# A two-layer graph network: layer 1 sums its messages in bfloat16, as three exact pieces side by side

## The chip, the core and the metric

The kernel runs on one core of one Trainium2 chip. The metric is the device time of one execution in microseconds (us), lower is better. Before the change three runs took 4851.73, 4855.97 and 4856.16 us; the median is 4855.97 us.

The engines are named as the profile names them: PE is TensorE (PEld its weight loads), DVE is VectorE, ACT is ScalarE, POOL is GpSimd, SP is SyncE.

## What is computed

Two message-passing layers over a graph of 6250 nodes and 200000 edges, sorted by target. `src` is an edge's source node and `dst` its target. Cut to what matters:

```python
h = relu(layernorm(x))                              # (6250, 128)
# layer 1: attention with 8 heads of 16 numbers
z = (h @ W).reshape(N, 8, 16)
e = leaky_relu(el[src] + er[dst], 0.2)              # el, er: one number per node and head
a = exp(e - emax[dst])
agg = segment_sum(z[src] * a[:, :, None], dst)      # the sum that is changed
out = agg / segment_sum(a, dst)[:, :, None] + bias
x = x + out
# layer 2: per-edge products of a node's row with edge attributes and a small MLP of the
# edge's features, again summed by target, and a linear map; x = x + that
```

## The kernel before

The edges are cut into 196 groups of 1024 (8 columns of 128 edges, one edge on each partition). Both layers walk the 196 groups in 49 rounds of 4 (slots s = 0 to 3). A group's work in layer 1 is as follows.

- **POOL** gathers the source rows of the group: 8 indirect DMAs (line 436), each of 128 rows of 144 float32 numbers, from the table `z_tab` in DRAM into `rows`, slot s. A row holds, per head, 16 numbers of z and a 1 (so that the same sum gives the denominator), in all MW = 136 numbers, and 8 numbers `el`. Before the 8 gathers of group g it waits (line 461) until PE has signalled `agg` of group g - 2, the summing matmuls below. In this layer POOL does nothing else.
- **PE** copies the targets' numbers out over the partitions (`spread`, line 1161, two matmuls of 512 columns), two groups ahead; **ACT** turns this into a transposed one-hot (lines 527 and 530); **PE** fetches the targets' `er` with it (line 1170, 8 small matmuls, signalled as `er`), also two groups ahead.
- **DVE**, once the rows have landed: adds `el` and `er` (941, 942), takes the maximum (946), writes the one-hot of the *next* group (862: 128x1024), and, once **ACT** has taken the exponential (551), forms the message in two halves of 4 columns (956: 128x544 each), signalled as `msg0` and `msg1`. Then it reduces the next group's `er` (869) and adds the previous group's sums from PSUM into an accumulator in SBUF (876: 128x136).
- **PE** sums: for each of the 8 columns a matmul with the one-hot of 128x128 float32 as weights and 136 columns of the message (1213). The last one signals `agg`.

After slot 1 of a round DVE finishes those blocks of 128 nodes that are complete (`finish_block`, lines 886 to 916, 49 in all, about one in a round): divide, add to x, layernorm, a transpose and a matmul on PE (1184, 1187), each of which DVE waits for (910, 915). The row goes to the table `up_tab` for layer 2, which SP stores.

Layer 2 has the same frame (8 gathers a group, from `up_tab`), with DVE products (1052 to 1069) and its own sums on PE (1278). It can't begin to gather before the last block of layer 1 has been stored.

The order on each engine is the order in which it is written; nothing plans it. Each engine runs its own loop, and semaphores tie them.

Of the kernel before, what the change touches and what calls it, by code (L numbers as in the profile page):

```python
# [8 lines left out]
BF16 = mybir.dt.bfloat16  # L9
# [4 lines left out]
P = 128  # L14
# [51 lines left out]
def gnn_kernel(nc, x, src, dst, dst_lin, edge_y, edge_f, bias, front, weights, out):  # L66

    with ExitStack() as ctx:
# [31 lines left out]
        acc = sb("acc", [P, 4 * COLS])  # L100
# [18 lines left out]
        hotT = lay(U * GE, GE).bitcast(BF16).rearrange("p (h e) -> p h e", h=2)  # L119
# [14 lines left out]
        assert PARTS_AT + 2 * GE <= 4 * COLS and (U + 1) * GE <= COLS  # L134
# [77 lines left out]
        msg = part(0, 2, T, MW)  # L212
# [47 lines left out]
        def slot_sems(tag, names):  # L260
# [5 lines left out]
                                                         "exp", "msg0", "msg1", "agg", "added", "rows"))  # L266
# [342 lines left out]
        def _(dve):  # L609
# [251 lines left out]
            def one_hot(s, group):  # L861
                v.tensor_tensor(hot[:, s, :, :],  # L862
                                bc(dst_col[:, bass.ds(group, 1), :].rearrange("p a t -> p (a t)"), 2, P),
                                bc(iota_l1, 1, T), ALU.is_equal)
# [8 lines left out]
            def add_sums(s, at):  # L873

                to = sums_at[:, bass.ds(at, 1), :].rearrange("p a f -> p (a f)")
                v.tensor_tensor(to, to, bank[2 + s % 2][:, 0:MW], ALU.add).then_inc(s_l1["added"][s], 1)
# [43 lines left out]
            with dve.Fori(0, passes1) as k:  # L920
# [5 lines left out]
                v.memset(bank[3][:, 0:MW], 0.0)  # L926
                with dve.Fori(0, GI) as q:
                    n = dve.snap(k * GI + q + 1, min_val=1, max_val=PASSES1 * GI)
                    m = dve.snap(k * QUADS + q + 1, min_val=1, max_val=PASSES1 * QUADS)
                    m_1 = dve.snap(k * QUADS + q + 2, min_val=2, max_val=PASSES1 * QUADS)  # L930
                    landed = dve.snap(q * (16 * T) + 16 * T, min_val=16 * T, max_val=GI * 16 * T)
# [4 lines left out]
                    for s in range(U):  # L936
# [17 lines left out]
                        for hf in range(2):  # L954
                            ts = slice(hf * HT, hf * HT + HT)
                            v.scalar_tensor_tensor(  # L956
                                out=msg[:, h, ts, :].rearrange("p t (h f) -> p t h f", f=RW),
                                in0=bc(a_ps[h][:, ts, :], 3, RW), scalar=1.0,
                                in1=rows[:, s, ts, 0:MW].rearrange("p t (h f) -> p t h f", f=RW),
                                op0=ALU.min, op1=ALU.mult).then_inc(s_l1["msg0" if hf == 0 else "msg1"][s], 1)  # L960
# [7 lines left out]
                        add_sums((s - 1) % U, slots[s])  # L968
# [6 lines left out]
                add_sums(3, last)  # L975
# [125 lines left out]
        def _(pe):  # L1101
# [90 lines left out]
            with pe.Fori(0, passes1) as k:  # L1192
# [7 lines left out]
                with pe.Fori(0, GI) as q:  # L1200
# [5 lines left out]
                    for s in range(U):  # L1206
# [3 lines left out]
                        for i in range(T):  # L1210
                            if i % HT == 0:
                                pe.wait_ge(s_l1["msg1"][s] if i else s_l1["msg0"][s], n)
                            mm = t.matmul(bank[2 + h][:, 0:MW], hot[:, s, i, :], msg[:, h, i, :],  # L1213
# [154 lines left out]
```

## Time and profile before

| | |
|---|---|
| median of the timed runs | 4855.97 us |
| the profiled execution | 4860.6 us, its span 4858.4 us |
| busy share of the span | POOL 62%, PE 58%, DVE 52%, PE weight loads 42%, ACT 21% |
| DMA engines | under 20% busy in both layers |
| layer 1's gathers | from about 0.12 ms to 2.42 ms |
| layer 2's gathers | from 2.45 ms to the end |

Shares of busy time are means over both layers. A gap before an instruction is printed in brackets with what ended it; "remote" and "another core or an unknown queue" both mean that the profile has no instruction of this core whose recorded end fits. The ends of matmuls are modelled.

### The profile page before, as it was taken

The page shows a single profiled execution, that of the slowest core. Times are in us where ns is not written, and L with a number is a line of the kernel's source. Part 1 is how long each engine was busy: PE and PEld are TensorE (multiplying, and loading weights), DVE is VectorE, ACT ScalarE, POOL GpSimd, SP SyncE. Part 2 cuts the span into 40 slices and gives each one's busy share as a digit, 9 for nine tenths or more (in the row PEclk, how much of TensorE's full clock was granted, in tenths as well). Part 3 has the DMA queues.
Part 4 walks back from the last instruction along what each step waited for, and adds up shares of the span by engine and source line. Part 5 has one row for each costly group of instructions (what it writes and reads, how often), then busy time and mean ns, then how long its engine had stood idle before and what let it go on. Part 6 is the DMA issues. An engine that isn't in the chain of part 4 may idle for free.

```text
span 4858.4 us, 43517 instructions
## 1 busy us (share of the span) xinstructions
PE 2816.5 (58%) x11218; PEld 2050.7 (42%) x11219; DVE 2517.3 (52%) x6576; ACT 1018.9 (21%) x1447; POOL 3030.4 (62%) x3146
## 2 busy tenths in 40 slices
PE   2444444444444444444467777777777777777776
PEld 2333333333333333333345545455555554445454
DVE  7333333333434334333356666666666666666565
ACT  3222222222222222222221111111111111111111
POOL 2666666666666666666656666666666666666665
PEclk8665666566666566666678888888888888888888
DMA  3111111111111111111111111111111111111111
GB/s 104 50 51 49 52 49 52 52 52 48 52 52 51 52 53 51 52 52 50 50 43 51 47 49 46 49 48 50 49 51 49 49 50 48 47 49 49 47 47 39
DMA packets 139864, 246.43 MB, mean 51 GB/s; under 512 B 54124, under 2 KB 85974, under 8 KB 139734
## 3 DMA queue, kind: packets, MB, share of 16 engines
q0 software_dynamic: 100352, 218.57, 16.3%
q1 hardware_dynamic: 39352, 26.89, 1.9%
q10 hardware_dynamic: 144, 0.80, 0.1%
q8 instruction: 5, 0.08, 0.0%
q14 instruction: 11, 0.09, 0.0%
HBM read 236.02 MB, written 10.03 MB: 51 GB/s over the span
## 4 chain that ended last, share of the span: by engine, by line
POOL 41%; issue 21%; PE 15%; another core or an unknown queue 15%; DVE 4%; DMA 3%; ACT 1%; DVEq 0%; POOLq 0%; ACTq 0%; SPq 0%
POOL rows L436 41%; PE pair L1278 7%; PE pair L1240 2%; PE pair L1234 2%; DMA rows<-up_tab,idx 2%; PE pair L1230 1%; PE pair L1213 1%; PE pair L1254 1%; ACT share L565 1%; DMA rows<-z_tab,idx 0%; DVE share L1063 0%; DVE share L1057 0%; ACT share L567 0%; PE pair L1126 0%
## 5 line engine op out<-in xcount | busy, mean ns | idle before, releaser
L436 POOL DMA_INDIRECT rows<-up_tab,idx x1568 | 1534.1, 978 | 879.4 <-issue 473.1
L436 POOL DMA_INDIRECT rows<-z_tab,idx x1568 | 1494.9, 953 | 924.9 <-issue 557.4
L1213 PE MATMUL pair<-share,acc 128*128 128x136 f32 x3136 | 755.6, 432 | 1127.2 <-issue 653.8
L1213 PEld LDWEIGHTS pair<-share,acc 128*128 128x128 f32 x3136 | 701.1, 326 | 1263.8 <-issue 720.6
L1278 PE MATMUL pair<-share,acc 128*128 128x256 f32 x3136 | 933.5, 450 | 368.1 <-DVE share L1069 220.1
L1278 PEld LDWEIGHTS pair<-share,acc 128*128 128x128 f32 x3136 | 695.4, 228 | 764.6 <-issue 338.6
L941 DVE TENSOR_TENSOR share<-rows,share 128x64 f32<-128x64 f32 x196 | 46.0, 235 | 1159.2 <-DMA rows<-z_tab,idx 1152.8
L1052 DVE TENSOR_TENSOR share<-rows,y_sb 128x384 f32<-128x384 f32 x392 | 222.3, 567 | 631.9 <-DMA rows<-up_tab,idx 601.0
L1240 PE MATMUL pair<-weights_sb,share 128*128 128x256 f32 x1576 | 412.1, 408 | 130.5 <-ACT share L567 74.3
L1240 PEld LDWEIGHTS pair<-weights_sb,share 128*128 128x128 f32 x1576 | 313.0, 203 | 197.5 <-ACT share L567 87.8
L567 ACT ACTIVATE share<-pair,front_sb 128x512 f32<-128x512 f32 x198 | 136.1, 687 | 1046.3 <-issue 387.6
L551 ACT ACTIVATE pair<-share 128x64 f32<-128x64 f32 x196 | 44.6, 228 | 1441.7 <-DVE share L946 1132.9
L565 ACT ACTIVATE share<-pair,front_sb 128x512 f32<-128x512 f32 x198 | 136.1, 687 | 901.2 <-PE pair L1230 608.3
L1234 PE MATMUL pair<-share,weights_sb 128*128 128x512 f32 x396 | 264.1, 756 | 71.8 <-ACT share L565 71.1
L956 DVE SCALAR_TENSOR_TENSOR share<-pair,rows 128x544 f32<-128x544 f32 x392 | 264.1, 715 | 0.0
L996 DVE TENSOR_TENSOR acc<-acc,pair 128x1024 f32<-128x1024 f32 x197 | 239.8, 1217 | 1.4
L862 DVE TENSOR_TENSOR acc<-acc,pair 128x1024 f32<-128x1024 f32 x197 | 240.3, 1220 | 0.0
L1230 PE MATMUL pair<-ef_sb,weights_sb 64*128 64x512 f32 x396 | 235.9, 677 | 5.0 <-DMA ef_sb<-in_edge_f 4.2
L527 ACT ACTIVATE acc<-pair,acc 128x1024 bf16<-128x1024 f32 x198 | 219.7, 1110 | 90.7 <-remote 73.7
L530 ACT ACTIVATE acc<-acc,ones 128x1024 bf16<-128x1024 bf16 x198 | 227.3, 1148 | 6.4
L1057 DVE TENSOR_TENSOR share<-rows,share 128x384 f32<-128x384 f32 x392 | 219.3, 559 | 0.0
L1063 DVE TENSOR_TENSOR share<-share,y_sb 128x384 f32<-128x384 f32 x392 | 214.5, 547 | 0.0
(166 smaller groups left out, 2416.6 us busy)
## 6 DMA issues: line engine op xcount, KB each, us to landing
rows<-z_tab,idx POOLq DMA_INDIRECT x1568
rows<-up_tab,idx POOLq DMA_INDIRECT x1568
ef_sb<-in_edge_f SPq DMA_DIRECT2D x50, 128.0 KB
z_tab<-rows SPq DMA_DIRECT2D x7, 504.0 KB, 3.2
y_sb<-in_edge_y SPq DMA_DIRECT2D x50, 64.0 KB
x_sb<-in_x SPq DMA_DIRECT2D x7, 448.0 KB, 6.9
up_tab<-acc SPq DMA_DIRECT2D x49, 64.0 KB
out<-x_sb SPq DMA_DIRECT2D x48, 64.0 KB
```

The lines of the kernel that those rows point to most:

```text
L436: pool.indirect_dma_start(out=rows[:, s, t, 0:width], out_offset=None, in_=table, in_offset=bass.IndirectOffsetOnAxis(ap=indices[:, t:t + ...
L527: nc.scalar.activation(to, spread_ps, ACT.Square, bias=minus_id[:, bass.ds(tile, 1)])\
L530: nc.scalar.activation(to, to, ACT.Relu, bias=ones[:, 0:1], scale=-2.0).then_inc(s_l1["turned"][s], 1)
L862: v.tensor_tensor(hot[:, s, :, :], bc(dst_col[:, bass.ds(group, 1), :].rearrange("p a t -> p (a t)"), 2, P), bc(iota_l1, 1, T), ALU.is_equal)
L956: v.scalar_tensor_tensor(out=msg[:, h, ts, :].rearrange("p t (h f) -> p t h f", f=RW), in0=bc(a_ps[h][:, ts, :], 3, RW), scalar=1.0, in1=r ...
L996: v.tensor_tensor(hot[:, s, :, :], bc(dst_col[:, bass.ds(group, 1), :].rearrange("p a t -> p (a t)"), 2, P), bc(iota_l2, 1, T), ALU.is_equal)
L1052: v.tensor_tensor(vy, vecs, y_v, ALU.mult)
L1213: mm = t.matmul(bank[2 + h][:, 0:MW], hot[:, s, i, :], msg[:, h, i, :], start=(i == 0), stop=(i == T - 1))
L1230: t.matmul(bank[4], a1_bd[at, s, :], ef_sb[at, :], start=True, stop=True).then_inc(s_l2["h1"], 1)
L1234: t.matmul(bank[4], a2_bd[:, :], h1_sb, start=True, stop=True).then_inc(s_l2["h2"], 1)
L1240: mm = t.matmul(bank[2 * (s % 2) + j // 2][:, (j % 2) * 256:(j % 2) * 256 + 256], h2_sb[:, s % 2, j * P:(j + 1) * P], a3_bd[:, :], start=T ...
L1278: mm = t.matmul(bank[6 + s % 2][:, 0:MSG], hot[:, s, hf * HT + j, :], msg2[:, s % 2, hf, j, :], start=(hf + j == 0), stop=(hf == 1 and j = ...
```

## The change

Layer 1 only. The one-hot is written as bfloat16 (0 and 1 are exact in it). The float32 message m is split into three pieces, whose bits each fit a bfloat16: the upper half of m's own bits, the upper half of the rest, and the rest of that. The pieces lie side by side as `split[h]`, of shape [128, 3, 8, 136] float32 cells (2 buffers); `upper` is a view of the upper 2 bytes of each cell. Splitting takes four more DVE instructions a group, each reading two operands from `acc`, which is SBUF. `msg0` and `msg1` are signalled by the last two of them. PE then runs 8 matmuls of 3 x 136 = 408 bfloat16 columns, with a bfloat16 one-hot as weights. DVE adds the three sums (a reduction from PSUM into `part_sum`), and then adds that to the accumulator. Three core parts of the diff:

```diff
             def one_hot(s, group):
-                v.tensor_tensor(hot[:, s, :, :],
+                v.tensor_tensor(hot1[:, s, :, :],
...
-            def add_sums(s, at):
-
+            def add_sums(s, at, counted, wait=plain_wait):
+
+                v.tensor_reduce(part_sum, bank[2 + s % 2][:, 0:3 * MW].rearrange("p (c f) -> p f c", c=3), AX.X, ALU.add)\
+                    .then_inc(s_l1["folded"], 1)
                 to = sums_at[:, bass.ds(at, 1), :].rearrange("p a f -> p (a f)")
-                v.tensor_tensor(to, to, bank[2 + s % 2][:, 0:MW], ALU.add).then_inc(s_l1["added"][s], 1)
+                wait(dve, s_l1["folded"], counted)
+                v.tensor_tensor(to, to, part_sum, ALU.add).then_inc(s_l1["added"][s], 1)
...
-                        for hf in range(2):
-                            ts = slice(hf * HT, hf * HT + HT)
+                        by_half = [slice(0, HT), slice(HT, T)]
+                        for ts in by_half:
                             v.scalar_tensor_tensor(
-                                out=msg[:, h, ts, :].rearrange("p t (h f) -> p t h f", f=RW),
+                                out=split[h][:, 0, ts, :].rearrange("p t (h f) -> p t h f", f=RW),
                                 in0=bc(a_ps[h][:, ts, :], 3, RW), scalar=1.0,
                                 in1=rows[:, s, ts, 0:MW].rearrange("p t (h f) -> p t h f", f=RW),
-                                op0=ALU.min, op1=ALU.mult).then_inc(s_l1["msg0" if hf == 0 else "msg1"][s], 1)
+                                op0=ALU.min, op1=ALU.mult).then_inc(s_l1["halved"], 1)
+                        for hf, ts in enumerate(by_half):
+                            dve.wait_ge(s_l1["halved"], halves + (4 * s + hf))
+                            v.tensor_tensor(split[h][:, 1, ts, :], split[h][:, 0, ts, :], upper[h][:, 0, ts, :],
+                                            ALU.subtract).then_inc(s_l1["halved"], 1)
+                        for hf, ts in enumerate(by_half):
+                            dve.wait_ge(s_l1["halved"], halves + (4 * s + 2 + hf))
+                            v.tensor_tensor(upper[h][:, 2, ts, :], split[h][:, 1, ts, :], upper[h][:, 1, ts, :],
+                                            ALU.subtract).then_inc(s_l1["msg0" if hf == 0 else "msg1"][s], 1)
...
-                            mm = t.matmul(bank[2 + h][:, 0:MW], hot[:, s, i, :], msg[:, h, i, :],
+                            mm = t.matmul(bank[2 + h][:, 0:3 * MW], hot1[:, s, i, :], upper[h][:, :, i, :],
```

On DVE, in the loop of layer 1 from the messages of slot 2 to the start of slot 3, the order before is this (`pair2` holds the exponentials, `pair3` the er parts, `pair1` the sums, all in PSUM; `edges_` names the semaphores of the text above):

```order
L956 SCALAR_TENSOR_TENSOR share<-pair2,rows 128x544 [waits edges_exp_slot2]
L956 SCALAR_TENSOR_TENSOR share<-pair2,rows 128x544
L869 TENSOR_REDUCE share<-pair3 128x128 [waits edges_er_slot3]
L876 ISA [waits edges_er_sum_slot3]
L876 TENSOR_TENSOR acc<-acc,pair1 128x136
L941 TENSOR_TENSOR share<-rows,share 128x8x8 [waits edges_rows_slot3]
```

And in the same place of the changed kernel (its own line numbers; `acc` holds the pieces and the accumulator, `share` holds `part_sum`):

```order
L968 SCALAR_TENSOR_TENSOR acc<-pair2,rows 128x544 [waits edges_exp_slot2]
L968 SCALAR_TENSOR_TENSOR acc<-pair2,rows 128x544
L974 REGISTER_ALU
L975 TENSOR_TENSOR acc<-acc 128x544 [waits edges_halved]
L974 REGISTER_ALU
L975 TENSOR_TENSOR acc<-acc 128x544 [waits edges_halved]
L978 REGISTER_ALU
L979 TENSOR_TENSOR acc<-acc 128x544 [waits edges_halved]
L978 REGISTER_ALU
L979 TENSOR_TENSOR acc<-acc 128x544 [waits edges_halved]
L876 TENSOR_REDUCE share<-pair3 128x128 [waits edges_er_slot3]
L882 TENSOR_REDUCE share<-pair1 128x136 [waits edges_er_sum_slot3]
```

Four subtractions of two SBUF operands have come in between the messages and the er reduction, and behind it a reduction of the three sums (its add follows). Nothing else has changed places.

On PE, the summing of slot 2 before and, in the second piece, after:

```order
L1161 MATMUL pair0<-acc,pick 128x512 [waits edges_added_slot0]
L1213 MATMUL pair1<-share,acc 128x136 [waits edges_msg0_slot2]
L1213 MATMUL pair1<-share,acc 128x136 x3
L1213 MATMUL pair1<-share,acc 128x136 [waits edges_msg1_slot2]
L1213 MATMUL pair1<-share,acc 128x136 x3
L1170 ISA [waits edges_turned_slot0]
L1170 MATMUL pair3<-share,acc 128x48 x8
```

```order
L1181 MATMUL pair0<-acc,pick 128x512 [waits edges_added_slot0]
L1233 MATMUL pair1<-acc 128x408 [waits edges_msg0_slot2]
L1233 MATMUL pair1<-acc 128x408 x3
L1233 MATMUL pair1<-acc 128x408 [waits edges_msg1_slot2]
L1233 MATMUL pair1<-acc 128x408 x3
L1190 ISA [waits edges_turned_slot0]
L1190 MATMUL pair3<-share,acc 128x48 x8
```

The waits and their order are the same; only the shape and the type of the eight summing matmuls have changed.

## Rows read from the trace of the kernel before

**Rows 1.** Busy time by engine, steady part of layer 1 and of layer 2.

```profile
core 0: us, PE busy (x) PEld busy (x) DVE busy (x) ACT busy (x) POOL busy (x), PEclk, DMA share, GB/s
200.00:2350.00 2150.00, 917.43 (x4850) 760.07 (x4845) 817.70 (x1988) 579.46 (x723) 1372.88 (x1453) 0.62 0.19 51
```

**Rows 2.** Chain that ended last: start, us, what; at 1220 us.

```profile
1221.50 2.84 another core or an unknown queue
...
1224.38 0.78 issue
```

**Rows 3.** Timeline: start, us, engine, line, shapes, [idle before]; two groups of layer 1.

```profile
1213.04 0.28 DVE L941 TENSOR_TENSOR share<-rows,share 128x64 f32<-128x64 f32 x1 [9.22 <-DMA rows<-z_tab,idx]
...
1214.77 1.34 DVE L956 SCALAR_TENSOR_TENSOR share<-pair,rows 128x544 f32<-128x544 f32 x2
...
1215.54 4.00 PE L1213 MATMUL pair<-share,acc 128*128 128x136 f32 x16 [8.53 <-issue]
...
1216.03 0.55 DVE L869 TENSOR_REDUCE share<-pair 128x128 f32<-128x384 f32 x1
...
1216.81 0.94 POOL L436 DMA_INDIRECT rows<-z_tab,idx  x1 [0.31 <-issue]
...
1219.68 0.74 PE L1161 MATMUL pair<-acc,pick 114*128 114x512 bf16 x2
...
1224.75 1.35 DVE L956 SCALAR_TENSOR_TENSOR share<-pair,rows 128x544 f32<-128x544 f32 x2
1225.16 0.94 POOL L436 DMA_INDIRECT rows<-z_tab,idx  x1 [3.66 <-remote]
...
1232.62 0.35 DVE L915 TENSOR_SCALAR acc<-pair,share 128x128 f32 x1 [0.60 <-DVE share L912]
...
1236.39 0.28 DVE L941 TENSOR_TENSOR share<-rows,share 128x64 f32<-128x64 f32 x1 [3.42 <-DMA rows<-z_tab,idx]
```

**Rows 4.** Waits in layer 1, 200 to 2350 us: total us, times, longest us.

```profile
POOL rows L436 <- remote: 303.0, 88, 3.8
...
DVE share L910 <- remote: 77.6, 17, 13.2
...
POOL rows L436 <- PE pair L1213: 37.5, 6, 10.5
```

**Rows 5.** Instruction groups: busy us, mean ns | idle before; layer 1, 200 to 2350.

```profile
L436 POOL DMA_INDIRECT rows<-z_tab,idx x1453 | 1373.9, 946 | 777.4 <-issue 436.9 <-remote 303.0 <-PE pair L1213 37.5
...
L876 DVE TENSOR_TENSOR acc<-acc,pair 128x136 f32 x181 | 53.6, 296 | 29.4 <-DVE share L869 16.3 <-issue 13.1
```

**Rows 6.** The same view of layer 2, 2500 to 4800 us.

```profile
L436 POOL DMA_INDIRECT rows<-up_tab,idx x1512 | 1480.0, 979 | 821.8 <-issue 432.0 <-PE pair L1278 238.8 <-remote 150.9
...
L1063 DVE TENSOR_TENSOR share<-share,y_sb 128x384 f32<-128x384 f32 x378 | 206.8, 547 | 0.0
...
L1066 DVE TENSOR_TENSOR share<-share 128x128 f32<-128x128 f32 x378 | 105.8, 280 | 0.0
```

**Rows 7.** Timeline of layer 2: gathers beside DVE instructions with two SBUF inputs.

```profile
2463.01 0.55 DVE L1063 TENSOR_TENSOR share<-share,y_sb 128x384 f32<-128x384 f32 x1
2463.14 1.24 POOL L436 DMA_INDIRECT rows<-up_tab,idx  x1 [0.30 <-issue]
...
2464.67 0.61 DVE L1057 TENSOR_TENSOR share<-rows,share 128x384 f32<-128x384 f32 x1
2464.68 0.94 POOL L436 DMA_INDIRECT rows<-up_tab,idx  x1 [0.30 <-issue]
```

**Rows 8.** Timeline of layer 1: a late hand-over from PE to DVE, and POOL after it.

```profile
1084.21 0.47 PE L1184 MATMUL pair<-front_sb,share 128*128 128x128 f32 x1 [1.67 <-DVE share L908]
...
1097.39 0.29 DVE L910 COPY share<-pair 128x128 f32<-128x128 f32 x1 [13.24 <-remote]
...
1107.12 0.94 POOL L436 DMA_INDIRECT rows<-z_tab,idx  x1 [10.53 <-PE pair L1213]
```

**Rows 9.** Timeline: the first gather of layer 2.

```profile
2446.92 0.94 POOL L436 DMA_INDIRECT rows<-up_tab,idx  x1 [25.23 <-issue]
```

More of the change, by code:

```diff
@@ L99, in gnn_kernel @@
         x_sb = sb("x_sb", [P, NB, HIDDEN])
-        acc = sb("acc", [P, 4 * COLS])
+        acc = sb("acc", [P, 4 * COLS + 1350])
         max_acc = acc[0:HEADS, 0:COLS]
@@ L118, in gnn_kernel @@
         moved = lay(U * GE + 4 * P, P)
-        hotT = lay(U * GE, GE).bitcast(BF16).rearrange("p (h e) -> p h e", h=2)
+        hot1 = lay(0, U * GE // 2).bitcast(BF16).rearrange("p (u t n) -> p u t n", u=U, t=T)
+        hotT = lay(U * GE // 2, GE).bitcast(BF16).rearrange("p (h e) -> p h e", h=2)
         lin_i = lay(0, U * GE).bitcast(I32)
@@ L133, in gnn_kernel @@
         assert COLS + (NB + 1) * MSG <= AUX
-        assert PARTS_AT + 2 * GE <= 4 * COLS and (U + 1) * GE <= COLS
+        SPLIT_AT = (U * GE // 2 + GE, PARTS_AT + 2 * GE)
+        assert SPLIT_AT[0] + 3 * T * MW <= COLS and SPLIT_AT[1] + 3 * T * MW <= 4 * COLS + 1350
+        split = [lay(at, 3, T, MW) for at in SPLIT_AT]
+        upper = [x.bitcast(BF16).rearrange("p c t (f b) -> p c t f b", b=2)[:, :, :, :, 1] for x in split]
         dst_rel = sb("dst_rel", [P, NG, T])
@@ L210, in gnn_kernel @@
         dst_row = part(1024, GE, parts=1).bitcast(I32)
-        msg = part(0, 2, T, MW)
+        part_sum = part(0, MW)
         e_sb = part(2 * T * MW, 2, T, 2, HEADS)
@@ L265, in gnn_kernel @@
         s_l1 = named("edges", ("open",)) | slot_sems("edges", ("spread", "square", "turned", "er", "er_sum", "scored", "score",
-                                                         "exp", "msg0", "msg1", "agg", "added", "rows"))
+                                                         "exp", "msg0", "msg1", "agg", "added", "rows")) \
+            | named("edges", ("halved", "folded"))
         s_l2 = named("l2", ("h1", "h2", "tp", "first", "weighted", "dotted", "doubled")) | slot_sems("l2", ("h1_act", "h2_act")) \
@@ L925, in _ @@
                 one_hot(0, 0)
-                v.memset(bank[3][:, 0:MW], 0.0)
+                v.memset(bank[3][:, 0:3 * MW], 0.0)
                 with dve.Fori(0, GI) as q:
@@ L967, in _ @@
                             dve.wait_ge(s_l1["er_sum"][0], m_1)
-                        add_sums((s - 1) % U, slots[s])
+                        add_sums((s - 1) % U, slots[s], folds + s)
                         if s == 1:
@@ L974, in _ @@
                 dve.wait_ge(s_l1["added"][2], (k + 1) * GI + 1)
-                add_sums(3, last)
+                add_sums(3, last, (k + 1) * (NG + 1))
                 hold(dve, s_l1["added"][3], (k + 1) * QUADS)
```

2 lines of the change are left out of this document (added).

## The prediction

> **What bounds layer 1 now.** I read the busy time by stage first. In the steady part of layer 1 POOL is busy 1373 of 2150 us, PE 917 and DVE 818 [rows 1], so no engine is full and the chain of waits has to say who sets the pace. In it stand POOL's gathers, a short issue gap behind each, and behind every sixteenth gather a longer wait, here 1221.50 to 1225.16 [rows 2, 3]. A gather takes 0.946 us and the next starts 1.25 us after it, so two groups take 16 x 1.25 + 3.35 = 23.3 us, and 98 pairs are 2285 us: all of layer 1. DVE and PE are paced by it: DVE begins a group when its rows land (1213.04, 1223.08, 1236.39) and idles before that [rows 3].
>
> The long wait has no recorded end of this core's PE or DVE beside it: 303.0 us in 88 waits are put down to "remote", only 37.5 us in 6 waits to the summing matmuls [rows 4]. In the rows, PE's sums for the group in question ended at 1215.54 + 4.00 = 1219.54, before POOL was even through with its 16 gathers (1221.50); the wait went on until 1224.38, some 1.3 us after the last rows had landed. I take it for a wait for the drain of the gathers, which no engine's speed changes. So PE and DVE have slack: the sums end 5.6 us before the gather that needs them (1219.54 to 1225.16), for the other group of the pair it is as much: messages from 1224.75, sums until 0.77 + 4.0 later, 1229.5, and the gather that needs them is the ninth from 1225.16, at 1235.2 [rows 3].
>
> **The change on PE.** Before, 8 matmuls (16 records) take 4.0 us. After, 8 matmuls of 408 bfloat16 columns. The two bfloat16 matmuls of 512 columns at 1219.68 take 0.74 us, 0.36 us each, at a granted clock that is 0.62 of full in this stretch [rows 1, 3]; by columns that is 0.29 us for 408, at the lower of the two clock levels (1.2 GHz) 408 / 1.2 = 0.34 us. I take 8 x 0.34 = 2.7, with the tail 2.8 us: 1.2 us less a group. The pieces are read at every second bfloat16; if that halved the rate it would be 5.4 us, 1.5 us more than now. Either lies in the slack.
>
> **The change on DVE.** Two instructions of 128x384 and 128x128 float32 elements with both inputs in SBUF take 0.547 and 0.280 us [rows 6]: 1.04 ns an element. With 544 elements that makes 0.547 + 160 x 0.00104 = 0.71 us. Back to back they start 0.64 us apart, as the two of line 956 do (1.34 us for two of 0.71). Four subtractions: +2.55 us. The reduction of the three sums (408 elements) costs what the er reduction of 384 costs, 0.55 us [rows 3], and a hand-over of some 0.16 us: +0.7 us. The add itself stays at 0.296 us [rows 5]. DVE is busy 3.3 us more a group, 196 x 3.3 = 640 us in the layer, all under POOL's cover: 818/2150 is 4.4 of 11.65 us a group, and becomes 7.7. `msg0` comes 2.55 us later, PE takes 1.2 us less, so `agg` ends 1.35 us later; of 5.6 us of slack 4.2 are left. After slot 1 the finish of a block begins 3.3 us later. Before, it ended at 1232.97 with the next group at 1236.39, 3.4 us apart [rows 3]: it just fits.
>
> **The term that remains: POOL and DVE get in each other's way.** In layer 2 the gather that starts at 2463.14, while a DVE instruction with two SBUF inputs runs (2463.01 to 2463.56), takes 1.24 us in place of 0.945; the one at 2464.68, with such an instruction starting 0.01 us before it, 0.94 [rows 7]. So a gather whose start falls into such an instruction waits until 0.13 us before its end (2463.56 - 0.13 - 2463.14 = 0.29), unless it has practically started with it. Over layer 2 a gather takes 979 ns, in layer 1, where these instructions are tiny and the messages and one-hots have one input in PSUM, 946 [rows 5, 6]: 33 ns x 1568 = 52 us. The four subtractions have both inputs in SBUF and bring 2.55 us of such time, unbroken, into each group.
>
> Where they fall can be worked out. In the group of 1213.04 they would start at 1216.03 (where the er reduction started), 1216.67, 1217.31 and 1217.95, each 0.71 long. The gather at 1216.81 falls into the second: held until 1217.38 - 0.13, +0.44. The next, due at 1218.06 + 0.44 = 1218.50, falls into the last (to 1218.66): +0.03. In the other group (messages from 1224.75) they start at 1226.02, 1226.66, 1227.30, 1227.94. Gathers follow 1225.16 every 1.25 us [rows 3]: 1226.41 is held until 1226.73 - 0.13, +0.19; the next, at 1227.85, until 1228.01 - 0.13, +0.03. Mean (0.47 + 0.22) / 2 = 0.35 us a group, x 196 = 68 us. It hangs on the phase: with subtractions 0.2 us later the first group's gather at 1216.81 would start with one, untouched. The bounds are 0 (no hold) and random phase: 2.55 / 1.25 = 2.04 starts a group in such time, held for about 0.27 us each, 108 us. Nothing could make this term a gain. I take 60 us, near the two rows worked out, since the phase drifts by tenths.
>
> The Trainium skill ("SBUF — State Buffer", section "Who interferes with whom") speaks on both sides. It says that a DVE instruction with two SBUF inputs contends with a GpSimd instruction that reads SBUF, and also that such instructions had not been seen to stall GpSimd's DMAs, inferring that descriptors need only the write side. By the second this term would be nothing; rows 7 speak for the first.
>
> **Sum, against the profiled execution.** Hold +60. The 6 waits of POOL for `agg` [rows 4] come 1.35 us later each, or 4.7 where a finish stood before it: +12 (8 to 28). At the end of the layer POOL waits 25.23 us for the last blocks [rows 9]; this path has `agg` 1.35 later and one reduction more: +2. 4860.6 + 74 = 4935; the profiled execution is 4.6 us above the median of the runs, so I predict 4930.
>
> **Rivals.**
>
> *PE sets the long wait (the other side).* If the 3.66 us waits of POOL end with a signal of PE that reaches it late because of the fp32 sums, whose 16 passes run beside the gathers, then half as many instructions and 1.2 us less free it. For it: line 461 waits for `agg`, and nothing but that and the gathers is there to wait for; modelled ends can be wrong. Against: PE had idled since 1220.42 by its rows. Price: of 3.35 us extra in 98 pairs up to 3.3, 320 us; with the holds, 4930 - 320 = 4610; if only a third goes, 4825. It decides from the point where `agg` reaches POOL before 1221.50.
>
> *No hold.* The subtractions don't hold gathers: 4856 + 14 = 4870, and without the smaller terms 4856. Against: rows 7. For: layer 2's stretched gathers could come from its PSUM readers.
>
> *The finish falls late.* At 1084.21 PE transposes; DVE takes it over 12.7 us later, and POOL then waits 10.53 us in place of 3.5 [rows 8]: 7 us lost. DVE's takeover is late 17 times, 77.6 us in all [rows 4], but mostly by 1 to 3 us, inside the slack. Later by 3.3 us, it moves against the gathers by 2.6 places, past all that the trace shows, and the slack behind it is down from 3.4 to 0.1 us. If a third to all of the 49 blocks then cost 7 to 9 us, that adds 120 to 400: 5050 to 5330. Against: most takeovers now are immediate.
>
> *It doesn't do what it says.* Strided pieces double PE's time: `agg` 4 us later, still within 5.6, and the 6 waits longer: 4950. It moves into the forecast's range.
>
> **How the numbers follow.** Chances: forecast 0.60, PE sets the wait 0.11, no hold 0.10, late finish 0.16, slow PE 0.03. The forecast's own range is 4890 to 4985 (holds 25 to 108 with the other terms). The range reaches down to 4856 (no hold) and up to 5080 (the cheaper half of the late finish), leaving out the first rival and the dear part of the third. About 0.2%, 10 us, is what a measurement of this kernel can tell from no change. Faster: the first rival, 0.11. Within 0.2%: half of no hold and a little of the forecast's lower end, 0.08. Slower: 0.81.
>
> **What would show it.** Right: layer 1's gathers at a mean of about 985 ns instead of 946, long ones starting inside a subtraction; the wait behind every sixteenth gather still near 3.5 us; layer 2 unchanged at 979 ns and in length; subtractions of 0.71 us; PE's sums in 2.8 us; the first gather of layer 2 some 72 us later. Wrong: gathers still at 946 ns (no hold); long waits of POOL gone or short (PE set them); many waits of 7 to 10 us with a late takeover at line 910's copy (finish); sums of 5 us (strided reads).

## The result

The changed kernel takes 4990.06 us (median of four runs, 4976.02 to 5003.53), the kernel before 4856.07 us (median of four, 4851.73 to 4887.35): ratio 1.0261, 95% interval 1.0225 to 1.0298. It is slower by 134 us; 4930 was predicted, with 4856 to 5080 as the range. The profiled execution is the longest of the four (5003.53 us, span 5001.7). Ratios, here and below, compare only executions within 1.5% of their kernel's fastest, since a kernel's executions at times fall into two groups; for c_after that leaves two of its four, for e_after three, for e_late_and_hold two.

First the starts of the gathers, which cut the span into stages. This is the view of one line, of the changed kernel: ns minimum/median/maximum, then first and last start.

```profile
L443 POOL DMA_INDIRECT rows<-z_tab,idx x1568: 942/947/7323, 90.3 to 2522.5; - x196
L443 POOL DMA_INDIRECT rows<-up_tab,idx x1568: 942/947/1441, 2560.2 to 4970.3; - x196
```

The same view of the kernel before:

```profile
L436 POOL DMA_INDIRECT rows<-z_tab,idx x1568: 939/945/7323, 88.5 to 2420.8; - x196
L436 POOL DMA_INDIRECT rows<-up_tab,idx x1568: 939/947/1332, 2446.9 to 4834.2; - x196
```

So of the 143 us between the two spans, layer 1 (first to last start) has 2432.2 - 2332.3 = 99.9, the way to layer 2 has 37.7 - 26.1 = 11.6, layer 2 has 2410.1 - 2387.3 = 22.8, and 9.0 lie behind the last gather and ahead of the first. Layer 2's part can't be put down to the change: its code is the same, and on another chip (runs e_before and e_after below) layer 2 was 17.8 us shorter with the change.

In layer 1 the gathers themselves are longer. Instruction groups of the changed kernel, 200 to 2350 us (busy, mean ns | idle before), beside [rows 5]:

```profile
L443 POOL DMA_INDIRECT rows<-z_tab,idx x1390 | 1364.1, 981 | 790.5 <-issue 419.2 <-PE pair L1233 224.6 <-remote 146.8
L1233 PE MATMUL pair<-acc 128*128 128x408 bf16 x1395 | 500.3, 535 | 1044.9 <-issue 627.1 <-DVE acc L979 417.8
L979 DVE TENSOR_TENSOR acc<-acc 128x544 bf16<-128x544 f32 x350 | 246.3, 756 | 0.0
L975 DVE TENSOR_TENSOR acc<-acc 128x544 f32<-128x544 f32 x350 | 238.6, 723 | 0.0
L882 DVE TENSOR_REDUCE share<-pair 128x136 f32<-128x408 f32 x174 | 101.4, 583 | 6.0
```

981 ns in place of 946. Over the whole layer the page of the profile has 1550.6 us for the 1568 gathers of layer 1, and 1494.9 before: 55.7 us of the 99.9. The other 44 are idle time of POOL, and its waits have changed their kind. (This part differs from chip to chip. In the profiled pairs of the experiments below the gathers of layer 1 are longer by 62.4 us, c_after, and 63.1 us, e_after, but POOL's idle time between them is 82 us longer in c_after, an execution of 5142 us, and 9 us shorter in e_after.) Waits of the changed kernel in the same stretch (total us, times, longest), beside [rows 4]:

```profile
ACT acc L534 <- remote: 295.3, 39, 11.5
POOL rows L443 <- PE pair L1233: 224.6, 35, 18.9
POOL rows L443 <- remote: 146.8, 43, 4.4
DVE share L920 <- remote: 93.2, 10, 10.6
DVE share L876 <- remote: 70.1, 18, 6.6
```

POOL's waits put down to "remote" are halved (303.0 in 88 to 146.8 in 43), and waits that do end with TensorE's sums have come up, 37.5 in 6 to 224.6 in 35. The regular picture of a long wait behind every 16 gathers [rows 2, 3] is gone. POOL's timeline of the changed kernel, without the gathers that followed at 0.3 us:

```profile
1222.21 0.94 POOL L443 DMA_INDIRECT rows<-z_tab,idx  x1 [4.36 <-remote]
1234.96 0.95 POOL L443 DMA_INDIRECT rows<-z_tab,idx  x1 [3.00 <-PE pair L1233]
1269.70 0.94 POOL L443 DMA_INDIRECT rows<-z_tab,idx  x1 [3.69 <-remote]
1281.84 0.95 POOL L443 DMA_INDIRECT rows<-z_tab,idx  x1 [2.37 <-PE pair L1233]
```

Between 1234.96 and 1266.00 lie 24 gathers in one run, between 1222.21 and 1231.95 eight. So the wait isn't something that 16 gathers in a row bring with them.

**A held gather.** Timeline of the changed kernel (start, duration):

```profile
1006.51 0.94 POOL L443 DMA_INDIRECT rows<-z_tab,idx  x1 [0.30 <-issue]
1007.10 1.35 DVE L975 TENSOR_TENSOR acc<-acc 128x544 f32<-128x544 f32 x2
1007.76 1.51 POOL L443 DMA_INDIRECT rows<-z_tab,idx  x1 [0.30 <-issue]
```

The second of the two subtractions starts at 1007.73 and ends at 1008.45; the gather of 1007.76 takes 1.51 us, some 0.56 too much, so it was held until 0.13 us before that end, as worked out from [rows 7].

**A late hand-over.** Timeline of the changed kernel: TensorE's transpose for the finish of a block, VectorE's takeover, the next group's sums, and the gather that waits for them.

```profile
1168.51 0.47 PE L1204 MATMUL pair<-front_sb,share 128*128 128x128 f32 x1 [3.23 <-DVE share L918]
1175.56 0.29 DVE L920 COPY share<-pair 128x128 f32<-128x128 f32 x1 [7.11 <-remote]
1177.25 0.95 POOL L443 DMA_INDIRECT rows<-z_tab,idx  x1 [0.30 <-issue]
1182.94 1.40 DVE L979 TENSOR_TENSOR acc<-acc 128x544 bf16<-128x544 f32 x2
1183.75 2.90 PE L1233 MATMUL pair<-acc 128*128 128x408 bf16 x8 [6.20 <-DVE acc L979]
1187.48 0.95 POOL L443 DMA_INDIRECT rows<-z_tab,idx  x1 [9.28 <-PE pair L1233]
```

The transpose's record is at 1168.51; VectorE got word of it at 1175.56. The group behind the finish is then late, its sums end at 1186.65, and POOL stands still for 9.28 us. The step to layer 2 has one such hand-over too, and it accounts for the 11.6 us there (36.75 us of waiting for 25.23 [rows 9]):

```profile
2526.75 0.29 DVE L920 COPY share<-pair 128x128 f32<-128x128 f32 x1 [10.72 <-remote]
...
2560.23 0.95 POOL L443 DMA_INDIRECT rows<-up_tab,idx  x1 [36.75 <-issue]
```

### The profile page after: what moved, and what is told of

Its sections match the earlier page's. It is cut to its first block, busy times and chain, and to the rows that moved or that the text cites. A ratio compares the mean times of both kernels' runs of the same rounds, so it can differ in the third digit from the quotient of the medians.

```text
span 5001.7 us, 42343 instructions
## 1 busy us (share of the span) xinstructions
PE 2679.8 (54%) x9650; PEld 1583.3 (32%) x9651; DVE 3137.2 (63%) x7557; ACT 1017.9 (20%) x1447; POOL 3071.9 (61%) x3146
## 4 chain that ended last, share of the span: by engine, by line
POOL 28%; issue 22%; PE 19%; another core or an unknown queue 16%; DVE 8%; DMA 4%; ACT 2%; DVEq 1%; ACTq 0%; POOLq 0%; SPq 0%
POOL rows L443 28%; PE pair L1298 8%; PE pair L1254 3%; PE pair L1260 3%; PE pair L1233 2%; DMA rows<-z_tab,idx 2%; PE pair L1250 2%; DMA rows<-up_tab,idx 1%; DVE acc L979 1%; DVE acc L968 1%; ACT share L572 1%; PE pair L1274 1%; DVE acc L869 1%; PE pair L1207 0%
## 5 line engine op out<-in xcount | busy, mean ns | idle before, releaser
L443 POOL DMA_INDIRECT rows<-z_tab,idx x1568 | 1550.6, 989 | 971.0 <-issue 560.6
L1233 PE MATMUL pair<-acc 128*128 128x408 bf16 x1568 | 562.4, 535 | 1164.8 <-issue 699.8
L1298 PEld LDWEIGHTS pair<-share,acc 128*128 128x128 f32 x3136 | 694.8, 228 | 735.6 <-issue 334.1
L1233 PEld LDWEIGHTS pair<-acc 128*128 128x128 bf16 x1568 | 195.0, 135 | 1546.5 <-issue 993.1
L1260 PE MATMUL pair<-weights_sb,share 128*128 128x256 f32 x1576 | 430.6, 422 | 130.9 <-ACT share L574 69.0
L979 DVE TENSOR_TENSOR acc<-acc 128x544 bf16<-128x544 f32 x392 | 275.9, 757 | 0.0
L968 DVE SCALAR_TENSOR_TENSOR acc<-pair,rows 128x544 f32<-128x544 f32 x392 | 264.4, 716 | 12.3 <-ACT pair L558 10.0
L975 DVE TENSOR_TENSOR acc<-acc 128x544 f32<-128x544 f32 x392 | 267.2, 723 | 0.0
L1016 DVE TENSOR_TENSOR acc<-acc,pair 128x1024 f32<-128x1024 f32 x197 | 239.9, 1218 | 1.3
L869 DVE TENSOR_TENSOR acc<-acc,pair 128x1024 bf16<-128x1024 f32 x197 | 240.2, 1219 | 0.0
```

What stands on the lines that cost most here:

```text
L443: pool.indirect_dma_start(out=rows[:, s, t, 0:width], out_offset=None, in_=table, in_offset=bass.IndirectOffsetOnAxis(ap=indices[:, t:t + ...
L869: v.tensor_tensor(hot1[:, s, :, :], bc(dst_col[:, bass.ds(group, 1), :].rearrange("p a t -> p (a t)"), 2, P), bc(iota_l1, 1, T), ALU.is_equal)
L968: v.scalar_tensor_tensor(out=split[h][:, 0, ts, :].rearrange("p t (h f) -> p t h f", f=RW), in0=bc(a_ps[h][:, ts, :], 3, RW), scalar=1.0, ...
L975: v.tensor_tensor(split[h][:, 1, ts, :], split[h][:, 0, ts, :], upper[h][:, 0, ts, :], ALU.subtract).then_inc(s_l1["halved"], 1)
L979: v.tensor_tensor(upper[h][:, 2, ts, :], split[h][:, 1, ts, :], upper[h][:, 1, ts, :], ALU.subtract).then_inc(s_l1["msg0" if hf == 0 else ...
L1016: v.tensor_tensor(hot[:, s, :, :], bc(dst_col[:, bass.ds(group, 1), :].rearrange("p a t -> p (a t)"), 2, P), bc(iota_l2, 1, T), ALU.is_equal)
```

## The experiments

The theory after this comparison: a "remote" wait is a wait for a signal of TensorE that arrives late while gathers run (late means: after the end of TensorE's record, and the ends of these records are modelled); the change costs by held gathers, and by moving VectorE's and TensorE's work to places among the gathers where the signals come late. The rivals: the drain of the prediction; TensorE's wider sums as the cost; VectorE's load alone.

The kernels ran in four sets, each on another chip, and chips differ more than the change does: the kernel before took 4957, 4300, 4870 and 4944 us in them. Ratios are to the kernel before on the same chip. All runs carry one addition, which asserts the bounds of the two numbers of a loop, and whose own price the controls c_before and e_before give:

```
-                ready[0:1, bass.ds(at, 2)], engines=(kind,), min_val=0, max_val=NB - 1,
-                skip_runtime_bounds_check_because="they are sums of flags over NB - 1 blocks")
+                ready[0:1, bass.ds(at, 2)], engines=(kind,), min_val=0, max_val=NB - 1)
```

### First set: two controls, no subtractions, release by the messages

**c_before and c_after**: only that edit, on the kernel before and on the changed one.

> The kernel before, with the same assertions and nothing else. Expected within 0.3% of before (4856 us), gathers 0.946 us. If the assertions cost, it shows here: 49 rounds in each layer, each 0.1 us on an engine that waits, would be 5 to 10 us.

Measured 1.0063 (1.0040 to 1.0086). The assertions cost a little more than I said.

> The changed kernel, with one addition: the bounds of the finish's loop (one pair of numbers for each of four engines in every round of four groups) are asserted after they are loaded, 49 rounds in each layer. Control for the others. If the assertions are free: ratio to before 1.022 to 1.030 (about 4990 us), layer 1's gathers 0.98 us in the mean. If they are not: a longer time, from longer idle before the first instruction behind them.

Measured 1.0252 (1.0182 to 1.0323), within the interval of the first chip's 1.0261.

**c_no_subtract**: the changed kernel less its four subtractions.

```
-                        for hf, ts in enumerate(by_half):
-                            dve.wait_ge(s_l1["halved"], halves + (4 * s + hf))
-                            v.tensor_tensor(split[h][:, 1, ts, :], split[h][:, 0, ts, :], upper[h][:, 0, ts, :],
-                                            ALU.subtract).then_inc(s_l1["halved"], 1)
...
-                            v.tensor_tensor(upper[h][:, 2, ts, :], split[h][:, 1, ts, :], upper[h][:, 1, ts, :],
...
+                for x in split:
+                    v.memset(x[:, 1:3, :, :].rearrange("p c t f -> p (c t f)"), 0.0)
```

> The changed kernel without its four subtractions in each group: the second and third pieces stay zero, so TensorE multiplies as many columns as in the changed kernel and the reduction of three sums stays, but only the upper 16 bits of the messages are summed. Theory (the subtractions cost, by holding gathers and by giving the messages 2.5 us later): gathers back to 0.946 us, few waits of over 7 us, 4856 us give or take 15. Rival (TensorE's wider bfloat16 sums or the reduction cost): stays above 4930 us.

Measured 1.0131 (1.0091 to 1.0171): with the 0.6% of the assertions, neither of the two. The gathers are back to their length (951 ns in the mean of the whole layer, as in c_before with 952), and of the 1.9% that c_after lies above c_before the subtractions make 1.2, give or take 0.8 by the two intervals. 0.7% over the control stays, but of the 48 us between the two profiled spans only 19.7 lie in layer 1; 26.7 lie in layer 2, whose code is the same. So what TensorE's wider sums and the reduction cost in layer 1 is 0.4% in one pair of profiles, with VectorE's messages given as early as ever. The waits have changed their kind here too. c_no_subtract, 100 to 1650 us:

```profile
ACT acc L533 <- remote: 323.2, 33, 12.1
POOL rows L442 <- remote: 161.0, 34, 5.2
DVE share L875 <- remote: 148.9, 23, 9.8
POOL rows L442 <- PE pair L1225: 114.0, 29, 16.8
```

and c_before:

```profile
POOL rows L435 <- remote: 226.1, 61, 4.1
ACT acc L526 <- remote: 70.2, 65, 6.6
DVE share L868 <- remote: 0.8, 1, 0.8
```

With shorter sums, TensorE signals at other places among the gathers. ScalarE then waits less often but far longer (323.2 us in 33 for 70.2 in 65), and VectorE, which had hardly such a wait, has 23. And TensorE's sums being ready sooner didn't bring POOL's release sooner: over the layer's 53 "remote" waits of POOL of over 1.5 us ahead of a group, the sums had ended 3.0 us before POOL's last gather did, and the signal came 4.3 us after that gather (medians, counted in the trace).

**c_msg_release**: the kernel before, POOL in layer 1 waiting for the messages in place of `agg`.

```
+                        v.memset(part(3212, 1), 0.0).then_inc(freed, 1)
...
-                            hold(pool, s_l1["agg"][(s + AHEAD) % U], n)
+                            if by_messages:
+                                made = pool.snap(done * NG + q * U + (s + 1), min_val=1, max_val=PASSES1 * NG)
+                                hold(pool, freed, made)
```

> The kernel before, but in layer 1 a gather's wait is for VectorE's messages of two groups back (a one-element memset behind them gives the signal) and no longer for TensorE's sums of that group; the slot that it writes was last read four groups back, by VectorE. Theory A (TensorE's signal reaches GpSimd late, and that makes the long waits of 3.4 us in every second group): they shrink to the 1.2 us of the others, layer 1 loses some 150 to 230 us, total 4630 to 4710. Theory B, the prediction's (the long wait is a drain of 16 gathers that no engine's speed changes): they stay, 4856 us. Between: VectorE's own waits for TensorE take over, 4720 to 4820.

Measured 1.0634 (1.0593 to 1.0676), 5269 us: slower by 6%, where both theories saw no loss. It is the run that taught most. Its waits, 100 to 1650 us:

```profile
ACT acc L531 <- remote: 656.4, 45, 22.0
DVE share L874 <- remote: 492.5, 26, 19.7
POOL rows L436 <- DVE share L967: 402.3, 54, 16.2
```

Freed of TensorE's signal, POOL runs on, and now the signals that ScalarE and VectorE need come late. The timeline shows one:

```profile
1210.89 0.33 PE L1191 MATMUL pair<-front_sb,share 128*128 128x128 f32 x1 [1.56 <-issue]
...
1219.60 0.94 POOL L436 DMA_INDIRECT rows<-z_tab,idx  x1 [0.30 <-issue]
1223.63 0.29 DVE L915 COPY share<-pair 128x128 f32<-128x128 f32 x1 [12.80 <-remote]
```

TensorE's transpose is short and alone. POOL went on until 1220.54, and the signal came 3.1 us after that, 12.4 after the transpose. Of the 49 such transposes of layer 1, 7 ended when POOL had stood still for over 5 us, and VectorE started 0.04 us after them. The other 42 ended while gathers ran: VectorE started 1.7 to 3.3 us after 37 of them, mostly with POOL still gathering, and 8.2 to 12.7 us after five. So a signal can get through between gathers, but late.

A pause doesn't let a signal through at once either. This is e_before (the kernel before with the assertions, third set), where POOL's last gather ended at 1184.59 and the transpose 0.66 us later:

```profile
1183.56 1.03 POOL L435 DMA_INDIRECT rows<-z_tab,idx  x1 [0.30 <-issue]
1184.92 0.33 PE L1183 MATMUL pair<-front_sb,share 128*128 128x128 f32 x1 [2.06 <-issue]
1187.38 0.29 DVE L909 COPY share<-pair 128x128 f32<-128x128 f32 x1 [2.52 <-remote]
1188.05 0.94 POOL L435 DMA_INDIRECT rows<-z_tab,idx  x1 [3.46 <-remote]
```

In that trace 17 transposes end 0.66 to 0.95 us after POOL's last gather, and VectorE starts 2.7 to 3.05 us after that gather in all 17. POOL's own waits look alike. In the kernel before, 92 of its "remote" waits ahead of a group are over 1.5 us: the sums had ended some 2.0 us (median) before POOL's last gather did, and the signal came 2.5 to 3.05 us after that gather in 84 of them. So in this kernel the long wait's end follows POOL's last gather and not TensorE's sums; the regular 3.4 us wait is a pause in which TensorE's signals arrive. Signals aren't always late beside gathers: in c_before 32 of the 49 transposes end among gathers and are taken over after 0.04 us or so. What decides it the runs don't show.

### Second set: VectorE's load, the hold, and late messages apart

The kernel before, with four idle instructions in each group. **d_hold** (two inputs in SBUF) and **d_load** (one in PSUM) have them behind the message signals; **d_late_messages** has d_load's ahead of them.

```
+                        for rep in range(2):
+                            for hf in range(2):
+                                ts = slice(hf * HT, hf * HT + HT)
+                                v.tensor_tensor(spare[rep][:, hf, :, :], rows[:, s, ts, 0:MW], rows[:, s, ts, 0:MW], ALU.subtract)
```

In d_load and d_late_messages the instruction in the loop is

```
+                                v.scalar_tensor_tensor(
+                                    out=spare[rep][:, hf, :, :].rearrange("p t (h f) -> p t h f", f=RW),
+                                    in0=bc(a_ps[h][:, ts, :], 3, RW), scalar=1.0,
+                                    in1=rows[:, s, ts, 0:MW].rearrange("p t (h f) -> p t h f", f=RW),
+                                    op0=ALU.min, op1=ALU.mult)
```

> The kernel before (with the asserted bounds), and in layer 1 four idle subtractions in each group behind the message signals: both inputs are the gathered rows in SBUF, 128x544 float32, about 0.72 us each; nothing reads what they write. Theory (a gather that starts inside such an instruction is held): gather mean 0.946 to about 0.98 us, layer 1 longer by 50 to 70 us, ratio to before 1.016 to 1.024 with the 0.6% of the assertions. If only VectorE's load counts, the gathers stay at 0.946 and this run equals the next one. Rival: nothing, 1.006.

> As the last, but the four idle instructions are copies of the message's own form: one input in PSUM, one in SBUF, 0.71 us each. Theory of the hold: gathers stay at 0.946 us; what is left is VectorE's 2.6 us more for each group behind the signals: 1.006 to 1.012. If the finish of a block, which begins 2.6 us later, already costs here (its transpose's signal then falls in a run of gathers): some waits of over 7 us ahead of the first group of a round, 1.010 to 1.020.

> As the last (PSUM and SBUF inputs, 0.71 us each), but the four stand ahead of the message signals, so that TensorE gets the messages 2.6 us later, as in the changed kernel, and no gather is held. If the messages' lateness costs by itself (TensorE's sums and its signals fall later in the run of gathers): 10 to 15 waits of over 7 us and layer 1 longer by 30 to 90 us, 1.012 to 1.025. If slack takes it in, as predicted (5.6 us of it, 2.6 used): as the last run, 1.006 to 1.010.

Measured 1.0287 (1.0264 to 1.0311), 1.0203 (1.0181 to 1.0226) and 1.0463 (1.0442 to 1.0483). Gathers, 200 to 2100 us, in this order:

```profile
L437 POOL DMA_INDIRECT rows<-z_tab,idx x1406 | 1403.1, 998 | 497.9 <-issue 391.3 <-PE pair L1218 106.6
```

```profile
L437 POOL DMA_INDIRECT rows<-z_tab,idx x1440 | 1363.7, 947 | 536.4 <-issue 423.2 <-PE pair L1222 113.2
```

```profile
L437 POOL DMA_INDIRECT rows<-z_tab,idx x1364 | 1288.1, 944 | 613.4 <-issue 411.7 <-PE pair L1224 201.7
```

The hold is shown: the same place and nearly the same length (0.72 and 0.71 us), and only the run whose four have two SBUF inputs lengthens the gathers, by 51 ns. It costs 0.8% (layer 1 from first to last start 2129.7 against 2079.0 us). Messages that come 2.6 us later cost more: 118 us of layer 1 (2197.4), 2.6% of the time, 109 of it in waits for TensorE's sums (231.6 us over the layer for 122.3). VectorE's load alone (d_load, 1.4 to 1.7% over the controls, which ran on other chips) was to be hidden too, and isn't. My figures for all three were too low. This chip is the one of the four on which the kernel before takes 4300 us, and in the traces of this set's four kernels there is not one wait put down to "remote", in either layer (in d_load VectorE starts 0.04 us after each of the 49 transposes, gathers or none). Of d_load's 97 places behind 16 gathers POOL is idle for under 1 us at 54, and the waits at the others end with TensorE's recorded sums, so the same gathers bring no fixed wait with them. I take it that POOL has no pauses here in which a cost on VectorE could hide; the kernel before itself has no trace on this chip, so this isn't shown.

**d_after_no_finish**: the changed kernel, with `finish_block`, `std_block` and `map_up` called for all 49 blocks behind the groups.

```
-                            blocks(dve, mybir.EngineType.DVE, q + 1, finish_block)
+                            pass
...
-            last_blocks(dve, finish_block)
+            last_blocks(dve, finish_block, 0)
```

> The changed kernel (with the asserted bounds) whose 49 finishes of blocks are all made behind layer 1's groups and none among them. Only layer 1's own span is to be compared; the 49 finishes add some 300 us behind it (6 us each). If the long waits of the changed kernel come from the finish being late: none over 7 us ahead of the first group of a round, and the span from the first to the last gather falls from 2433 us to 2260 to 2340. If they come from TensorE's late signals at large, finish or none: 2400 or more.

Measured 1.0791, with the 49 finishes behind layer 1 as said. The layer's span came out shorter than I had room for; my figures were for a chip with late signals. Whole layer:

```profile
L446 POOL DMA_INDIRECT rows<-z_tab,idx x1568 | 1573.7, 1004 | 596.7 <-issue 584.3 <-PE pair L1236 12.4
```

Layer 1 is 2082.3 us, with one wait over 7 us. On this chip, then, without finishes among its groups the changed kernel has the longer gathers and hardly a wait for the sums (12.4 us). What the whole changed kernel costs here, and what the kernel before takes without its finishes, was not measured.

### Third set: the change beside VectorE's half of it

**e_after** and **e_before** are the two controls again. **e_late_and_hold** is the kernel before with d_hold's four subtractions ahead of the message signals: TensorE's sums in float32 and no second reduction.

> The changed kernel with asserted bounds again, beside its parts on one chip. The first set ran where TensorE's signals come late while gathers run (waits put down to 'remote' in the trace, before 4957 us), the second where none does (before 4300 us). Theory: where none comes late, the change costs by the held gathers (some 75 us) and by messages that come 2.6 us later (d_late_messages less d_load: 114 us), so 1.04 to 1.055; where they come late, the pauses hide part: 1.022 to 1.032. Rival (the change's cost is one for every chip): 1.025 either way.

> Kernel before with asserted bounds: 1.002 to 1.008. Where no signal comes late, layer 1's span is 1990 to 2030 us, near 1568 gathers at 1.25 us (1960 us); where they do, 2330 to 2345 us with 97 waits of 2 to 7 us.

> Kernel before with four idle subtractions (two SBUF inputs, as in the change) ahead of the message signals: VectorE's and GpSimd's side of the change, with TensorE's sums in float32 as before and no second reduction. If the subtractions explain the whole change: within 0.5% of e_after. If TensorE's shorter sums give something back: e_after lies below this run, by up to 1.2 us for each group that is waited for (up to 230 us in all if every group's sums are on the path; 30 to 100 us expected). If the reduction and the wider sums cost: e_after lies above it.

Measured 1.0204 (1.0091 to 1.0317), 1.0033 (1.0004 to 1.0061), and for e_late_and_hold 4953.65 and 4909.01 us in the two executions compared, mean 4931, against 4961 for e_after's three and 4869.55 of before. e_after came out just under the 1.022 to 1.032 that I gave for a chip with late signals, and its interval takes in the rival's 1.025, so it decides nothing between them. The four executions of each lie 1.7 and 2.1% apart (4909 to 4993, 4938 to 5040). In the profiled executions layer 1 is 40.0 us longer than e_before's 2334.8 in e_late_and_hold, and 54.5 us in e_after. In these profiles, then, VectorE's half gives most of layer 1's loss; whether TensorE's half adds the rest isn't resolved. Gathers of the whole layer, e_before, e_after, e_late_and_hold:

```profile
L435 POOL DMA_INDIRECT rows<-z_tab,idx x1568 | 1495.2, 954 | 926.2 <-issue 551.5 <-remote 328.1 <-PE pair L1212 46.5
```

```profile
L442 POOL DMA_INDIRECT rows<-z_tab,idx x1568 | 1558.3, 994 | 919.8 <-issue 568.8 <-PE pair L1232 181.0 <-remote 169.9
```

```profile
L437 POOL DMA_INDIRECT rows<-z_tab,idx x1568 | 1554.8, 992 | 907.9 <-issue 543.4 <-remote 190.5 <-PE pair L1220 173.9
```

The two kernels with subtractions have nearly the same hold, 63 and 60 us, and the same exchange of "remote" waits for waits that end with the sums. On this chip that exchange is even: POOL's idle time is no longer than before (919.8 and 907.9 us for 926.2), so in these profiles layer 1 lost no more than the hold.

### Fourth set: fewer gathers

**f_half_gathers**: the kernel before, with four gathers for each group of layer 1; the other half of its rows is stale.

```
-                for t in range(T):
+                for t in range(n):
...
-            gather_edges(z_tab, ZW, 0)
+            gather_edges(z_tab, ZW, 0, T // 2)
```

> The kernel before (asserted bounds), with four of the eight gathers of each group in layer 1 left out (the other half of the rows is stale; layer 2 is whole). GpSimd then has 5 us of gathers for each group, and VectorE and TensorE set the pace. Theory (TensorE's signals are late only while gathers run without a pause, on a chip that has this at all): in layer 1 hardly a wait put down to 'remote' (under 20 us, where c_before and e_before have more), and in layer 2 of the same run as many as before (some 300 us on each of ScalarE's two activations). Rival (a chip's TensorE signals late whatever GpSimd does): the same share of late ones in layer 1. On a chip without late signals neither layer shows any, and the run tells nothing. Layer 1 then takes 196 groups at 7 to 9 us, 1400 to 1800 us, and the whole 3900 to 4300 us on the slower chips.

4223.48 us, two runs. Waits, 100 to 1650 us:

```profile
POOL rows L436 <- PE pair L1213: 609.4, 115, 16.3
ACT acc L527 <- PE pair L1161: 189.8, 99, 2.9
DVE acc L915 <- remote: 67.6, 23, 4.0
DVE share L910 <- remote: 43.9, 15, 4.9
ACT acc L527 <- remote: 7.5, 6, 4.3
```

The theory holds in the main: POOL has no "remote" wait left (226.1 us in 61 in c_before over the same stretch), ScalarE 7.5 us for 70.2. It is not under 20 us in all, as I said, but 119: the finish still falls among gathers, and its two hand-overs are late 38 times, with waits of no more than 4.9 us. Layer 2 of the same run, with all its gathers, has as many as layer 2 of c_before (373.8 us in 35 and 305.9 in 30):

```profile
ACT share L565 <- remote: 375.6, 33, 15.7
ACT share L567 <- remote: 297.8, 28, 13.0
```

## Why the prediction was right, and where not

- **The number.** 4990 lies inside the range, 4856 to 5080, but above the forecast's own 4890 to 4985; what covers it is the room that the late finish was given. The direction was forecast with 0.81. The step from 4930 to 4990 is mostly waits that the sum had nearly at nothing, and by e_after's profile these waits can also come to nothing, so that the total came out near is in part luck of the chip. A smaller slip: 98 pairs of 23.3 us make 2285 of layer 1's 2332 us between its first and last gather, not all of it.
- **The hold.** Predicted +60 us, gathers at about 985 ns; measured +55.7 and 989 over the layer. The mechanism (d_hold against d_load), its form (the 1.51 us gather) and its size are right. Of the 1560 gathers behind the first group, I count 339 in the trace that start inside a subtraction (over 0.02 us behind its start and 0.13 ahead of its end); they take 1.106 us in the mean, the others 0.947, which makes 54 us. The Trainium skill ("SBUF — State Buffer", section "Who interferes with whom") has it that such VectorE instructions weren't seen to stall GpSimd's DMAs; the trace disagrees, by these 0.16 us for each, and bears out the other side of that page, which the prediction gives. Before the change, 183 gathers start inside a message product, which has one input in PSUM (counted in the same way), and take 0.944 us: no hold there.
- **The instructions.** Subtractions 0.723 and 0.756 us for 0.71, reduction 0.583 for 0.55, eight matmuls 2.9 us for 2.8. Reading every second bfloat16 costs nothing to speak of: TensorE's busy time is 0.88 ns a column for these 408, and 0.92 for the 512 contiguous ones of the spread, in the same stretch. Rival four falls.
- **"A wait for the drain of the gathers, which no engine's speed changes."** This step failed in its second half. The wait does end at a nearly fixed time after POOL's last gather (2.5 to 3.05 us in 84 of 92). But what it waits for is `agg`, as line 461 says and the first rival had it in part, and it isn't bound to 16 gathers, nor out of the engines' reach: the second chip runs the same gathers without it, the changed kernel has runs of 24 (the sign "behind every sixteenth gather still near 3.5 us" failed), and with TensorE's signal out of POOL's way (c_msg_release) or half the gathers POOL has no "remote" wait at all. The first rival's price fell too: shorter sums don't bring the signal sooner (c_no_subtract), and without the wait it is ScalarE and VectorE that stand (c_msg_release).
- **The slack of 5.6 us, and "+12" for the waits for `agg`.** The slack was read up to the gather behind a late-signal wait. On the chip where signals are prompt, 2.6 us of lateness cost 118 us (d_late_messages). Here POOL's idle time grew by 44 us in layer 1 and 11.6 behind it, for +12 and +2 in the sum: 42 of the 69 us by which the profiled execution's 143 pass the 74 of the sum. The hold gives 4 back, layer 2 has 23, the two ends of the program 9.
- **VectorE's 3.3 us, "all under POOL's cover".** d_load adds 2.6 us behind the signals and costs 1.4 to 1.7% where no signal is late. That the cover was the long waits is my reading; no run has this load alone on a chip with late signals.
- **The late finish.** Given 0.16 and priced at 120 to 400 us, it came true in part. VectorE's takeover was late 10 times for 93.2 us where it had been 17 times for 77.6 [rows 4], so a late one now waits 9.3 us in the mean for 4.6, with next to nothing left of the 3.4 us behind a finish. Waits for the sums rose by 187 us, and "remote" waits gave 156 back; I had not seen that the two would offset.
- **Layer 2 unchanged.** 22.8 us longer in this profile, and 17.8 shorter on another chip: more likely scatter than cause. The first gather of layer 2 came 113 us later, for 72 forecast, by layer 1's waits and the late hand-over behind it.

What stays open: by what path gathers delay TensorE's signals, whether it is the signal or the end of the matmul that is late (the profile models these ends, and notes the transpose's semaphore of c_msg_release 12.4 us behind one), why one chip of those used doesn't show it, and what TensorE's half of the change costs. c_no_subtract puts it at 19.7 us of layer 1 on one chip, e_after beside e_late_and_hold can't resolve it. No run pointed to a version that beats both kernels.

## What to carry to other kernels

When a chain of waits has pieces with no owner ("another core or an unknown queue"), find out which semaphore the engine waited for, and compare its recorded arrival with the end of the work it stands for, before calling it a fixed cost; slack measured up to the end of such a wait isn't slack. VectorE work with two SBUF inputs isn't free beside GpSimd's indirect DMAs, even where VectorE is half idle: count the starts that fall inside it. And work put ahead of a signal costs by where the signal then falls, so ask what stands directly behind it in the tightest place of the round (here the finish), not in the mean.

## What the runs showed of the hardware

- TensorE's signals to VectorE, ScalarE and GpSimd can arrive late while GpSimd issues indirect gathers, and just behind them: in c_msg_release 42 of 49 transposes were taken over 1.7 to 12.7 us late, and in e_before 17 that ended within 1 us of GpSimd's last gather were taken over 2.7 to 3.05 us after that gather. Where GpSimd had stood still for over 5 us (7 times in c_msg_release) they came within 0.04 us. They aren't late each time: in c_before 32 of 49 among gathers were prompt.
- On one of the chips none was late, in four kernels with the same gathers. The kernel before takes 4300 us on it and 4856 to 4957 on the others. Layer 2, the same code in every run, spans 2154 to 2157 us there and 2387 to 2521 on the others, with gathers of 966 to 968 ns there and 969 to 979 on the others. How much of this the late signals make isn't shown.
- On two chips with late signals the changed kernel's four executions lie 2% apart (5056 to 5159 us in c_after, 4938 to 5040 in e_after), on the first chip 0.6%; the four of d_load, on the chip without, 0.5%. Nothing here says why.
- A gather that starts inside a VectorE instruction with two SBUF inputs is held until some 0.13 us before its end (1.51 us for 0.95 in the row shown); one that starts inside an instruction with an input in PSUM is not (0.944 us in the mean of 183).
